# Rounding, weighing and scaling on GpSimd in two stages of a six-layer kernel

## What is computed

```python
# layer 1
q, k, v = (split_heads(t) for t in (x @ w_q, x @ w_k, x @ w_v))
attn = softmax(einsum('bnqd,bnkd->bnqk', q, k) * 64 ** -0.5)
o = einsum('bnqk,bnkd->bnqd', attn, v)
...
# layer 4, for each of 8 experts, of at most 512 rows
def act_quant(x):
    scale = 127.0 / max(max(abs(x), axis=-1), 1e-5)
    return clip(round(x * scale), -128, 127) / scale
def bitlinear(x, norm_w, w):
    return act_quant(rmsnorm(x, norm_w)) @ weight_quant(w).T
probs = softmax(bitlinear(rmsnorm(x), gate_in_norm_w, gate_w))
topw, topi = top_k(probs, 2)
h = bitlinear(rows_of_this_expert, gp_norm_w, gp_w)
g, y = split(h, 2, axis=-1)
out = bitlinear(silu(g) * y, dp_norm_w, dp_w)
```

## Time and profile before

| what | us |
|---|---|
| median of 3 runs | 2188.49 (2183.98 to 2189.59) |
| the profiled execution | 2170.81 |
| its span | 2169.0 |
| PE busy in it | 1670.8 (77%) |
| DVE busy | 1538.7 (71%) |
| ACT busy | 1447.3 (67%) |
| POOL busy | 761.0 (35%) |
| granted TensorE clock, share of full | 0.887 |

### The profile page before, as it was taken

The page is one execution under the profiler, slowest core; times in us unless marked ns, Lnnn a source line. Parts: engine busy times, 40 slices in busy tenths (PEclk is TensorE's granted clock), DMA queues, the critical chain, the costliest instruction groups (busy, mean ns, idle before and its releaser), DMA issues. The chain is left out here.

```text
span 2169.0 us, 43206 instructions
## 1 busy us (share of the span) xinstructions
PE 1670.8 (77%) x13315; PEld 1065.8 (49%) x13332; DVE 1538.7 (71%) x3296; ACT 1447.3 (67%) x2314; POOL 761.0 (35%) x733
## 2 busy tenths in 40 slices
PE   3889999999999999999479887222444579987677
PEld 1455555555555555555357765122222356665323
DVE  6877777787777777777443666574788478776765
ACT  2889989889898988989334665653556334442845
POOL 0444545555454545546200000455000355553000
PEclk9999999999999999999867988655667689998799
DMA  6223222223222222222142220172010411331002
GB/s 196 54 53 67 55 65 57 67 56 67 55 65 57 66 54 55 67 55 67 32 157 78 79 75 5 60 251 88 30 58 20 135 37 26 34 39 20 1 10 69
DMA packets 173818, 139.96 MB, mean 65 GB/s; under 512 B 83794, under 2 KB 155399, under 8 KB 173366
## 3 DMA queue, kind: packets, MB, share of 16 engines
q1 hardware_dynamic: 166710, 122.78, 21.2%
q0 software_dynamic: 6912, 14.71, 3.5%
HBM read 61.92 MB, written 20.97 MB: 38 GB/s over the span
## 5 line engine op out<-in xcount | busy, mean ns | idle before, releaser
L580 ACT ACTIVATE a_p_hi<-ps,a_probs_up,a_s_scale 128x512 f16<-128x512 f32 x512 | 397.8, 777 | 70.0 <-ACTq L578 69.2
L581 ACT ACTIVATE a_probs<-ps,a_probs_up,a_s_scale 128x512 f32<-128x512 f32 x512 | 397.6, 777 | 0.0
L695 DVE TENSOR_REDUCE a_top<-ps 128x2 f32<-128x1024 f32 x256 | 313.2, 1223 | 118.6 <-DVEq L694 118.5
L927 POOL TENSOR_TENSOR a_p_lo<-a_probs,a_p_hi 128x1024 f16<-128x1024 f32 x128 | 277.4, 2167 | 244.3 <-POOLq L926 201.8
L915 POOL TENSOR_TENSOR a_ops<-a_ident_down,a_top 64x256 f16<-64x256 f32 x256 | 159.8, 624 | 288.1 <-POOLq L910 279.6
L704 DVE TENSOR_TENSOR a_p_lo<-a_probs,a_p_hi 128x1024 f16<-128x1024 f32 x128 | 183.8, 1436 | 39.2 <-DVEq L703 39.2
L441 PE MATMUL ps<-a_ops 128*128 128x512 f16 x512 | 195.1, 381 | 14.6 <-PEq L439 14.3
L460 PE MATMUL ps<-a_v_hi,a_p_hi 128*128 128x65 f16 x2048 | 202.1, 196 | 4.4 <-PEq L455 4.2
L463 PE MATMUL ps<-a_v_lo,a_p_hi 128*128 128x64 f16 x2048 | 202.1, 194 | 0.0
L464 PE MATMUL ps<-a_v_hi,a_p_lo 128*128 128x65 f16 x2048 | 202.1, 195 | 0.0
L460 PEld LDWEIGHTS ps<-a_v_hi,a_p_hi 128*128 128x128 f16 x2048 | 189.1, 98 | 25.1 <-issue 14.2
(11 more groups left out here) (497 smaller groups left out, 3702.9 us busy)
## 6 DMA issues: line engine op xcount, KB each, us to landing
a_ops<-a_qk SPq DMA_DIRECT2D x384, 128.0 KB, 2.3
f_w<-in_L_ffn_W_dram SPq DMA_DIRECT2D x16, 1024.0 KB, 7.4
a_qd<-a_qk SPq DMA_DIRECT2D x128, 64.0 KB, 2.2
...
```

The costliest lines, as they stand in the source:

```text
L580: nc.scalar.activation(p_hi[:, h % 2, k, :], scores, ACT.Exp, bias=probs_up[:], scale=s_scale[:])
L581: nc.scalar.activation(probs[:, h % 2, k, :], scores, ACT.Exp, bias=probs_up[:], scale=s_scale[:]).then_inc(st_taken, 1)
L695: nc.vector.tensor_reduce(top[:, c % 2, 2 * pair:2 * pair + 2], ps[:, ROW:ROW + 2, :], AX.X, ALU.max).then_inc(row_taken, 1)
L927: nc.gpsimd.tensor_tensor(p_lo[:, h % 2, 2:KT, :], probs[:, h % 2, 2:KT, :], p_hi[:, h % 2, 2:KT, :], ALU.subtract).then_inc(p_made_pool, 1)
```

## The change

Three things are changed.

In self attention ACT no longer makes `p_hi` for the fourth key tile. POOL makes it, by a copy from `probs` that rounds to f16, ahead of its own subtraction and behind the same wait.

The gate has three parts of 3, 3 and 2 sequences (12, 12 and 8 tiles). Part 1 is now chosen and given its places in the last steps of `middle`; its sends, with those of part 2, still stand in the weights' stage, in POOL's list: 24, then 16.

In the experts' stage the buffers and loads of the first two experts' rows, and of `up_n`, are moved into the weights' stage. `a` has two buffers. POOL multiplies the rows with `up_n` for an expert two ahead, scales and rounds the rows of the next one, and multiplies tiles 0 and 1 of the hidden rows with `down_n`. DVE keeps the peaks, and does `rows(e + 1)` ahead of `hidden(e, 0)`; the peak of tiles 0 and 1 comes after tile 2. SP's loop is written out.

```diff
@@ self attention, powers on ACT; rest on POOL
-                    nc.scalar.activation(p_hi[:, h % 2, k, :], scores, ACT.Exp, bias=probs_up[:], scale=s_scale[:])
+                    if k < KT - 1:
+                        nc.scalar.activation(p_hi[:, h % 2, k, :], scores, ACT.Exp, bias=probs_up[:], scale=s_scale[:])
...
                     pool.wait_ge(probs_ready_pool, 1)
                     pool.sem_inc(probs_ready_pool, -1)
+                    nc.gpsimd.tensor_copy(p_hi[:, h % 2, KT - 1, :], probs[:, h % 2, KT - 1, :])
+                    pool.drain()
@@ the gate
-    SEQUENCES = (3, B - 3)
+    SEQUENCES = (3, 3, B - 6)
...
-    CHOICE = gate.SEQUENCES[0] - 1 + GATES
+    EARLY_PARTS = len(gate.SEQUENCES) - 1
+    CHOICE = [sum(gate.SEQUENCES[:h + 1]) - 1 + GATES for h in range(EARLY_PARTS)]
...
+                    if b in CHOICE[1:]:
+                        gate.power(act, CHOICE.index(b))
                     if 0 <= b - QUANTISE < B:
                         experts_rows(b - QUANTISE)
@@ the weights' stage
+                    sp.dma_start(up_n[:], row_of(up_norm)).then_inc(up_loaded, 16)
+                    sp.wait_ge(gate.sent, 16 * K * NT)
+                    for e in range(2):
+                        load(sp, e, e)
...
-                    gate.send(pool, REST)
+                    for part in range(1, REST + 1):
+                        gate.send(pool, part)
@@ the experts' stage, POOL
+                    def weigh_rows(e):
+                        pool.wait_ge(x_loaded[e % 2], 16)
+                        pool.sem_inc(x_loaded[e % 2], -16)
+                        nc.gpsimd.tensor_tensor(a[:, e % 2], x_in[:, e % 2], up_n[:, e, :].unsqueeze(1).broadcast_to([P, RT, D]), ALU.mult)
+                        pool.drain().then_inc(x_used, 1)
+                        pool.drain().then_inc(rows_weighed, 1)
+                    def scale_rows(e):
+                        pool.wait_ge(per_made, 1)
+                        pool.sem_inc(per_made, -1)
+                        for t in range(RT):
+                            nc.gpsimd.tensor_scalar(a[:, e % 2, t, :], a[:, e % 2, t, :], per_row[:, e % 2, t:t + 1], ROUND, ALU.mult, ALU.add)
+                        pool.drain().then_inc(a_round, 1)
+                    def weigh_hidden(e):
+                        pool.wait_ge(h_ready, 1)
+                        pool.sem_inc(h_ready, -1)
+                        nc.gpsimd.tensor_tensor(weighed[:, e % 2, 0:2, :], h[:, 0:2, :], down_n[:, e, :].unsqueeze(1).broadcast_to([P, 2, I]),
+                                                ALU.mult)
+                        pool.drain().then_inc(h_weighed, 1)
+                    weigh_rows(0)
+                    weigh_rows(1)
+                    scale_rows(0)
+                    for e in range(E):
+                        if e + 1 < E:
+                            scale_rows(e + 1)
+                        weigh_hidden(e)
+                        if e + 2 < E:
+                            weigh_rows(e + 2)
@@ the experts' stage, DVE
                     def expert(e, j, last):
+                        if not last:
+                            rows(e + 1, (j + 1) % 2)
                         hidden(j, 0)
                         hidden(j, 1)
-                        weigh(e, j, (0, 1))
-                        if not last:
-                            rows(e + 1, (j + 1) % 2)
+                        dve.drain().then_inc(h_ready, 1)
                         hidden(j, 2)
-                        weigh(e, j, (2,))
+                        weigh(e, j, 2)
+                        first_peaks(j)
                         hidden(j, 3)
-                        weigh(e, j, (3,))
+                        weigh(e, j, 3)
                         hidden_rows(e, j)
```

More of the change, by code:

```diff
@@ L1309, in middle @@
                 in_order += [("outT", b - 1, 0), ("outT", b - 1, 1)]
-            if b == CHOICE + 1:
-                in_order += [("counts",)]
+            if b - 1 in CHOICE:
+                in_order += [("counts", CHOICE.index(b - 1))]
             if b < B:
@@ L1620, in _ @@
                             outputs(b - 1, m)
-                    if b == CHOICE + 1:
+                    if b - 1 in CHOICE:
+                        part = CHOICE.index(b - 1)
                         pe.wait_ge(gate.kept_made, 1)
                         pe.sem_inc(gate.kept_made, -1)
-                        take(bank_of["counts",])
-                        gate.count(pe, 0, bank_of["counts",])
+                        take(bank_of["counts", part])
+                        gate.count(pe, part, bank_of["counts", part])
                     if b < B:
@@ L2057, in _ @@
                         gate_values(b - VALUES)
-                    if b == CHOICE + 1:
-                        gate.slots(dve, 0, bank_of["counts",], free[bank_of["counts",]])
+                    if b - 1 in CHOICE:
+                        bank = bank_of["counts", CHOICE.index(b - 1)]
+                        gate.slots(dve, CHOICE.index(b - 1), bank, free[bank])
                 dve.wait_ge(a_used, 2)
                 dve.sem_inc(a_used, -2)
-def quantise_rows(nc, dve, rows, peak, step, per_step, scale_tile):
-    nc.vector.tensor_reduce(peak, rows, AX.X, ALU.max, apply_absolute_value=True)
-    dve.drain()
-    nc.vector.tensor_scalar(peak, peak, 1e-5, None, ALU.max)
-    dve.drain()
-    nc.vector.reciprocal(per_step, peak)
-    nc.vector.tensor_scalar(step, peak, 1.0 / 127.0, None, ALU.mult)
-    dve.drain()
-    nc.vector.tensor_scalar(per_step, per_step, 127.0, None, ALU.mult)
-    dve.drain()
-    for t in range(TT):
-        part, factor = scale_tile(t)
-        nc.vector.tensor_scalar(part, part, factor, ROUND, ALU.mult, ALU.add)
-    dve.drain()
 class Routes:
@@ L2427, in _ @@
                     act.sem_inc(made, -1)
-                    whole(r[:], a[:], a_round, r_made)
+                    whole(r[:], a[:, 0], a_round, r_made)
                     rows_turned_out()
```

88 lines of the change are left out of this document (46 added, 42 removed).

## The result

The changed kernel takes 2201.4 us (median of 20 runs, 2187.0 to 2213.8), the kernel before 2189.2 us beside it (20 runs): ratio 1.0039, 95% interval 1.0021 to 1.0057. By the ratio it is 8.5 us slower, where 22.1 us less were forecast. A ratio here is estimated from all runs of a comparison and is not the quotient of the two medians, which lie 12.2 us apart; the interval, 4.6 to 12.5 us, holds both. Repeated later beside the experiments it was level with before (1.0000, 0.9970 to 1.0031). Neither interval reaches the forecast.

The account below looks back on a forecast made before the run. PE was taken to bound self attention, POOL to end the weights' stage, DVE to bound the experts. -5 - 6 - 3.9 - 7.2 = -22.1 us gave 2166.4 against the median of 2188.5; range 2150 to 2182.

Parts of the forecast that it names:

- Self attention, -5: Attention: 6 of PE's 14.3 us of waits for ACT come back, less POOL's copy delays; net -5 us (-14 to +12).
- DVE, which the change leaves alone there: Self attention: DVE taken as unchanged, though PE's waits for its row maxima are four times ACT's 14.3 us.
- The weights' stage, -6: Weights' stage, `middle` included: earlier sends let ACT end it near 1496 instead of 1502.1; -6 us (-10 to -1).
- The start of the experts, -3.9: Start of experts' stage: first rows ready after 8.1 us instead of 12.0; -3.9 us (-6 to -1).
- The experts, -7.2: Experts' stage: work moved from DVE to POOL, 20.2 us an expert instead of 21.0 for experts 1 to 5; -7.2 us in all.
- Rival 4: Self attention: POOL becomes the bound, PE waits for `p_lo`, kernel slower; 2221, or 2196 at half as many heads; chance 0.06.
- Rival 1: Experts' stage: the POOL and DVE lock eats the gain, 0 for one expert; 2173.6 us; chance 0.13.

Follow-up runs that it names:

- gate_alone: Kernel before with only the gate's choice in three parts: ratio to before 0.9968 (0.9949 to 0.9988).
- after_again: The whole changed kernel, unaltered, run again beside the experiments against the kernel before: ratio 1.0000 (0.9970 to 1.0031).
- experts_alone: Kernel before with only the experts' part: POOL weighs and scales rows, first rows loaded in the weights' stage; ratio 0.9969 (0.9950 to 0.9987).
- best: Changed kernel without the copy, POOL waiting in heads 0 and 13 for DVE's additions to X: 2148.3 us against before's 2175.8, ratio 0.9905.
- best_again: Changed kernel without the copy, with POOL's wait for DVE's additions to X, run a second time: 2178.6 us, ratio to before 0.9940.
- best_14: Changed kernel with POOL's wait for DVE's additions to X and the copy in 14 of 16 heads: 2171.3 us, ratio to before 0.9911.
- no_copy: Changed kernel without POOL's copy in attention, ACT making all the rounded powers: ratio to before 0.9932 (0.9907 to 0.9957).
- after_ordered: Changed kernel, copy kept, with POOL waiting in heads 0 and 13 for DVE's additions to X: ratio to before 0.9928 (0.9904 to 0.9951).
- before_ordered: Kernel before with only POOL's wait in heads 0 and 13 for DVE's additions to X: ratio to before 0.9932 (0.9899 to 0.9966).
- copy_ordered: Kernel before with the attention copy and POOL's wait in heads 0 and 13 for DVE's additions to X: ratio 0.9954 (0.9932 to 0.9976).
- relief: Kernel before without ACT's fourth-tile rounded powers, left at zero, and no copy: ratio to before 0.9987 (0.9966 to 1.0008).
- small_delay: Kernel before with one 128x160 write more on DVE behind head 0's additions to X: ratio to before 0.9998 (0.9973 to 1.0023).

## Why the prediction was wrong

*Self attention, -5: wrong in sign, +16.7.* The copy was sized well (0.86 against 0.8); the waits on ACT gave back 3.3 us of the 6. With the copy in 14 heads alone the net of -5 was measured as -5.9 in the trace and -7.8 by the ratio. The step that failed is "DVE, which the change leaves alone there". I had POOL's subtraction 0.24 us later and asked only who waits for its result, `p_lo`. I didn't ask which DVE instruction starts while it runs, though the earlier trace rows showed it at 438.11, and used that row for the experts alone. The term missing was the additions to X: 0.2 to 0.5 us more in head 1 in six sequences, up to 2.2 more in head 14 in five, and the clock's fall behind five of the first and two of the second, together 18.4 us in the trace. And I had the direction of the move right in head 1 only, where POOL ends later; in head 14 it comes earlier, as ACT is freed.

The Trainium skill has the rule (SBUF — State Buffer, "Who interferes with whom"): GpSimd and DVE share a port pair as a lock held for a whole instruction. The runs agree: 2.05 us with the lock, 0.48 with the order changed. That whoever issues first holds it, as the section has it, fits the trace too: the copy in front of head 1's additions, begun while DVE subtracts with two SBUF inputs, takes 0.78 us, and 0.61 where nothing is in its way.

```profile
442.73 1.47 DVE L705 TENSOR_TENSOR a_p_lo<-a_probs,a_p_hi 128x1024 f16<-128x1024 f32 x1 [0.25 <-DVEq L704]
443.89 0.78 POOL L928 CAST a_p_hi<-a_probs 128x512 f16<-128x512 f32 x1 [0.77 <-POOLq L927]
```

*The weights' stage, -6: right where it was measured alone.* `gate_alone` gives -7.0; in its trace `middle` is 2.0 us shorter, where I had it 2.3 longer, and the weights' stage 6.5. In the traces of after and `after_again` the two stages together are 13.0 and 18.5 us longer than before, not shorter; the last section has what is known of that. ACT ends the stage, as forecast. In the trace after, POOL's last send and ACT's last work:

```profile
1503.31 2.75 POOL L1199 DMA_INDIRECT expert_in<-gate_u,m_slot  x1 [0.30 <-issue]
```

```profile
1531.23 1.03 ACT L2221 ACTIVATE m_downT<-ps 128x1024 bf16<-128x1024 bf16 x1
```

The sends end 26 us before the stage does.

*The start of the experts, -3.9: right.* The first `hidden` came 19.3 us after the stage's start, now 15.4; the first rows were ready 8.1 us after it, as forecast (the terms of that sum make 8.0). The lock on DVE's small steps was there too, beside POOL's second product (0.17 us elsewhere):

```profile
1536.82 1.14 DVE L2554 TENSOR_SCALAR e_peak<-e_peak 128x4 f32<-128x4 f32 x1
```

*The experts, -7.2: right, a little large (6.2 in the trace after).* Stage after, DVE's third tile of one expert and of the next, the product between, and POOL's scaling:

```profile
1573.14 0.75 DVE L2569 SCALAR_TENSOR_TENSOR e_h<-ps,e_step,e_gated 128x512 f32<-128x512 f32 x1 [3.50 <-DVEq L2568]
1574.09 1.66 DVE L2575 TENSOR_TENSOR gate_u<-e_h,e_down_n 128x512 f32<-128x512 f32 x1 [0.20 <-issue]
...
1593.91 0.75 DVE L2569 SCALAR_TENSOR_TENSOR e_h<-ps,e_step,e_gated 128x512 f32<-128x512 f32 x1 [3.50 <-DVEq L2568]
```

```profile
1588.88 1.84 POOL L2369 TENSOR_SCALAR e_a<-e_a,e_per_row 128x256 f32<-128x256 f32 x4 [13.67 <-POOLq L2367]
```

DVE stands 3.50 us before tile 2 (3.4 forecast), the locked product takes 1.66 (1.9), the scaling 1.84 (1.8). From one hidden `whole` to the next pass 21.0, 20.6, 20.2, 20.8 and 20.2 us (20.2 forecast for all five). A collision that I left out is expert 0's, whose product of tile 2 is held for 2.81 us. Start and experts together: 10.1 us in the trace after and 9.7 in that of `experts_alone`, 6.7 by its ratio, 11.1 forecast.

*The rivals.* Rival 4 had the right side and a time near it, 2196, but that is luck, since its mechanism is another: its place, PE's wait for `p_lo`, rose by 1.3 us only. Rival 1's lock was the right cause in the wrong stage.

## What to carry to other kernels

When work is moved onto GpSimd, or its start moves by a few tenths, list the DVE instructions with two SBUF inputs that start while it runs, before and after, in every stage, and ask who waits for DVE then; a shift of 0.2 us cost 1.8 us in head 1. Look in the trace of before for one period that is longer than its likes: here one head in the sixth sequence showed the collision and the clock's fall that the change made common. And where two such instructions meet, an order between the engines (here POOL starts 1.5 us later) can be worth more than the relief of a busy engine: 14.9 us by the ratio, 9.5 in the trace, for one wait, and nothing that could be measured for some 80 us taken from ACT.

## What else the runs showed

**Slow issue around the sends.** `best` and `best_again` are the same kernel. DVE in the gate's last part in the first one (idle time ahead in brackets):

```profile
1411.38 0.23 DVE L1185 TENSOR_TENSOR gate_probs<-gate_probs,gate_hot 128x64 f32<-128x64 f32 x1
1411.68 0.23 DVE L1188 TENSOR_TENSOR gate_kept<-gate_kept,gate_probs 128x64 f32<-128x64 f32 x1
1411.98 0.22 DVE L1190 TENSOR_REDUCE gate_sums<-gate_kept 128x8 f32<-128x64 f32 x1
```

and in the second:

```profile
1435.83 0.23 DVE L1185 TENSOR_TENSOR gate_probs<-gate_probs,gate_hot 128x64 f32<-128x64 f32 x1 [0.50 <-issue]
1436.55 0.23 DVE L1188 TENSOR_TENSOR gate_kept<-gate_kept,gate_probs 128x64 f32<-128x64 f32 x1 [0.49 <-issue]
...
1439.42 0.23 DVE L1188 TENSOR_TENSOR gate_kept<-gate_kept,gate_probs 128x64 f32<-128x64 f32 x1 [1.26 <-issue]
```

The same steps stand 0.5 to 1.3 us each with nothing to wait for, and `middle` takes 357.6 us in place of 333.3. In the last 35 us of `middle` there are 9 to 11 such stands of DVE (over 0.35 us, with nothing to wait for, before a small step) in after, `after_again`, `best_14` and `best_again`, and at most 2 in the other 15 traces. All four have the gate in three parts, and come from comparisons in which the kernel before took 2187 to 2189 us; the four other kernels with three parts (`gate_alone`, `no_copy`, `best`, `after_ordered`) come from those with 2173 to 2176 us. From part 0's first send to the end of `middle` pass 51.0, 50.2, 49.8 and 51.1 us in the first four and 36.4 to 36.6 in the other four, so some 14 of the 15.4 us of `middle` in the trace after lie there, 9.3 of them in the stands counted. Kernels with two parts aren't spared: that stretch is 40.0 or 40.1 us in `before_ordered`, `copy_ordered` and `relief` and 47.5 in `small_delay`, all from comparisons with 2187 to 2189 us, and 33.8 to 34.5 in the traces of all the others (that of before, whose execution was the one of 2170.8 us, among them). So it may be that the third part's 7 us hold only in some conditions of the chip; after's loss of 8.5 us in its own comparison, against 1.9 by the parts, fits that, but no run tells the two apart. `best_again` gains less (0.9940) than `best` (0.9905), though their intervals overlap. What slows the issue was not tried.
